# Summing the four scan states of the third layer's attention on DVE instead of POOL

## The reference, cut to what matters

```python
def step(state, inp):
    d, b, c, u = inp
    dA = jnp.exp(d[..., None] * A)
    state = state * dA + (d * u)[..., None] * b[:, None, :]
    y = jnp.einsum('bdn,bn->bd', state, c)
    return (state, y)
...
y = y + D[None, :, None] * x
y = y * silu(z)
```

## Time and profile before

| | us |
|---|---|
| median of 3 runs | 1397.1 |
| lowest and highest | 1387.31 and 1399.21 |
| the profiled execution | 1404.3 |
| its span in the profile | 1402.6 |
| PE busy in the span | 1117.5 (80%) |
| DVE busy | 849.2 (61%) |
| POOL busy | 690.5 (49%) |
| ACT busy | 619.9 (44%) |

### The profile page before, as it was taken

One profiled execution on the slowest core, in us unless ns is written; L12 is line 12 of the kernel. 1 busy time (PEld: TensorE's weight loads), 2 busy tenths in 40 slices (PEclk: granted clock), 3 DMA queues, 4 the chain that ended last, 5 costly groups with the idle time before them and its releaser, 6 DMA issues.

```text
span 1402.6 us, 18531 instructions
## 1 busy us (share of the span) xinstructions
PE 1117.5 (80%) x5412; PEld 855.1 (61%) x5413; DVE 849.2 (61%) x1510; ACT 619.9 (44%) x1682; POOL 690.5 (49%) x457
## 2 busy tenths in 40 slices
PE   6766598777635887998998999759899635999993
PEld 4545476666323565777777777645555334888782
DVE  4475998979668853787878787922222564332222
ACT  4383355454451116786786867642111115333330
POOL 1005888887301213796886886810000003788874
PEclk9678899999767998999999999989999856999997
DMA  5572899986510003121221211055100397455556
GB/s 171 159 145 85 220 264 288 272 217 131 124 27 0 1 1 98 42 83 43 83 70 55 67 57 54 7 156 131 36 0 0 108 243 196 78 82 82 82 83 128
DMA packets 131233, 146.11 MB, mean 104 GB/s; under 512 B 29654, under 2 KB 115407, under 8 KB 131159
## 3 DMA queue, kind: packets, MB, share of 16 engines
q1 hardware_dynamic: 105494, 110.58, 27.5%
q0 software_dynamic: 24576, 33.57, 14.3%
q10 hardware_dynamic: 1088, 1.05, 0.2%
HBM read 119.04 MB, written 26.12 MB: 103 GB/s over the span
## 4 chain that ended last, share of the span: by engine, by line
PE 44%; issue 16%; POOL 11%; DVE 10%; DMA 7%; SPq 6%; ACT 5%; another core or an unknown queue 1%; DVEq 0%; ACTq 0%; POOLq 0%
PE bank L1967 5%; PE bank L1567 4%; PE bank L2260 4%; PE bank L1545 3%; POOL f_sums L927 3%; POOL arena L913 3%; PE bank L1487 3%; PE bank L1976 3%; PE bank L1578 3%; SPq L2146 3%; PE bank L1476 2%; POOL y L2182 2%; PE bank L1505 2%; DMA e_sums<-ctxT,put 2%; PE bank L1278 2%
## 5 line engine op out<-in xcount | busy, mean ns | idle before, releaser
L200 POOL TENSOR_TENSOR rstd<-var_eps,minus_half 128x8 f32<-128x8 f32 x8 | 13.2, 1647 | 304.8 <-DVE var_eps L192 304.8
L478 DVE TENSOR_TENSOR_SCAN arena<-arena 128x1024 f32<-128x1024 f32 x64 | 152.8, 2388 | 13.4 <-issue 5.8
L927 POOL DMA_INDIRECT f_sums<-arena,put x64 | 122.0, 1907 | 26.4 <-issue 16.5
L913 POOL DMA_INDIRECT arena<-y_rows,slots x64 | 84.7, 1324 | 77.3 <-DVEq L1122 58.1
L2260 PE MATMUL bank<-arena,ssm_y 128*128 x512 | 111.8, 362 | 2.4 <-issue 1.0
L2173 POOL DMA_INDIRECT e_sums<-ctxT,put x64 | 101.6, 1587 | 23.8 <-issue 16.5
L456 ACT ACTIVATE arena<-arena,ssm_A 128x255 f32<-128x255 f32 (+1 forms) x256 | 108.1, 503 | 1.8 <-DVE arena L428 1.8
L1693 ACT ACTIVATE arena<-bank,x_nb,x_rq 128x256 f32<-128x256 f32 x128 | 71.0, 560 | 82.1 <-DVE x_nb L1768 81.3
L1967 PE MATMUL bank<-yT,arena 128*128 128x512 f32 (+1 forms) x224 | 102.2, 600 | 0.0
L508 PE MATMUL bank<-arena,ident 128*128 128x256 f32 x256 | 70.3, 422 | 38.1 <-DVE arena L498 34.6
L2182 POOL DMA_INDIRECT y<-y_rows,slots x64 | 62.8, 982 | 74.1 <-DMA y_rows<-y 52.9
(11 more groups left out here) (321 smaller groups left out, 2802.1 us busy)
## 6 DMA issues: line engine op xcount, KB each, us to landing
arena<-bc_rows SPq DMA_DIRECT2D x64, 512.0 KB
arena<-in_L_ffn_w_gate_dram SPq DMA_DIRECT2D x16, 256.0 KB
arena<-in_L_ffn_w_up_dram SPq DMA_DIRECT2D x16, 256.0 KB
arena<-in_L_ffn_w_down_dram SPq DMA_DIRECT2D x16, 256.0 KB
x<-in_L_ffn_w_gate_dram SPq DMA_DIRECT2D x16, 256.0 KB
y<-in_L_ffn_w_up_dram SPq DMA_DIRECT2D x16, 256.0 KB
yT<-in_L_ffn_w_down_dram SPq DMA_DIRECT2D x16, 256.0 KB
arena<-in_L_ffn_Wd_dram SPq DMA_DIRECT2D x1, 3072.0 KB, 23.6
```

The lines of the kernel that those rows point to most:

```text
L478: nc.vector.tensor_tensor_scan(ssm_h[:, j % 2, :], ssm_decay[:, j % 2, :], ssm_in, 0.0, ALU.mult, ALU.add).then_inc(s_ssm_h, 1)
L913: nc.gpsimd.indirect_dma_start(out=f0_xg[:, n % RING, e, :], out_offset=None, in_=y_rows, in_offset=bass.IndirectOffsetOnAxis(ap=slots[:, ...
L927: nc.gpsimd.indirect_dma_start(out=f0_sums[m % SUMS], out_offset=bass.IndirectOffsetOnAxis(ap=put[:, m:m + 1], axis=0), in_=f0_ye[:, n % R ...
```

## The change

`ssm_out_pool` and `ssm_out_dve` go. POOL keeps only the product with C. DVE gets `ssm_reduce_dve` in every even step (b = 0 and 2): it sums the four states of the group before with one `tensor_reduce` (1024 elements in, 256 out; the four values of a sum lie 256 elements, 1024 bytes, apart) into `ssm_part`, and adds that to `ssm_y` with one addition of 256 elements. It stands after `add` and `krms` and ahead of `mixed_copy`. The last group's sum is done at the end of the layer, where `ssm_out_dve` stood. POOL's product into a half of `ssm_hC_buf` waits for the reduction that read that half, by the same semaphore as before (`s_ssm_red`); the semaphore of the additions, `s_ssm_red_y`, now counts 32 instead of 8.

```diff
-        def ssm_out_pool(pool, m, b, j):
+        def ssm_reduce_dve(dve, m, b, j):
 
             c = j % HC
             q = b * GB * HC + j
-            ssm_hC(pool, nc.gpsimd, m, b, j)
-            pool.wait_ge(s_ssm_hC, m * GROUPS + q + 1)
-            add = nc.gpsimd.tensor_tensor
-            both = ssm_hC_buf[:, j % 2, 0:2 * S]
-            add(both, both, ssm_hC_buf[:, j % 2, 2 * S:4 * S], ALU.add).then_inc(s_ssm_half[0], 1)
...
-        def ssm_out_dve(dve, m, b):
-
-            for c in range(HC):
-                dve.wait_ge(s_ssm_red, b * GB * HC + (GB - 1) * HC + c + 1)
-                row = ssm_y[:, m, ds(b, 1), c, :].rearrange("p a l -> p (a l)")
-                nc.vector.tensor_tensor(row, row, ssm_acc[:, c, :], ALU.add).then_inc(s_ssm_red_y, 1)
+            dve.wait_ge(s_ssm_hC, m * GROUPS + q + 1)
+            if not (isinstance(b, int) and b == 0 and j == 0):
+                dve.wait_ge(s_ssm_red_y, q)
+            nc.vector.tensor_reduce(ssm_part[:, :], ssm_hC_buf[:, j % 2, :].rearrange("p (n l) -> p l n", n=NB),
+                                    AX_X, ALU.add).then_inc(s_ssm_red, 1)
+            dve.wait_ge(s_ssm_red, q + 1)
+            row = ssm_y[:, m, ds(b, 1), c, :].rearrange("p a l -> p (a l)")
+            nc.vector.tensor_tensor(row, row, ssm_part[:, :], ALU.add).then_inc(s_ssm_red_y, 1)
...
                 if b == 0 and not beyond(h + 1):
                     krms(h + 1)
-                if b == 1 and k == 0 and not (isinstance(i, int) and i == 0):
-                    ssm_out_dve(dve, 1, i - 1)
+                if b % 2 == 0 and ago >= 2:
+                    j = 2 * k + b // 2
+                    ssm_reduce_dve(dve, 1, i if j else i - 1, j - 1 if j else GB * HC - 1)
                 if ago >= 1:
                     mixed_copy(s - 1, (b - 1) % B)
...
-            ssm_out_dve(dve, 1, B - 1)
+            ssm_reduce_dve(dve, 1, B - 1, GB * HC - 1)
...
-                ssm_out_pool(pool, 1, i, 2 * k)
+                ssm_hC(pool, nc.gpsimd, 1, i, 2 * k)
...
-                ssm_out_pool(pool, 1, i, 2 * k + 1)
+                ssm_hC(pool, nc.gpsimd, 1, i, 2 * k + 1)
```

More of the change, by code:

```diff
@@ L562, in gated_dve @@
                 norm_dve(dve, k)
-                dve.wait_ge(s_ssm_red_y, B * HC)
+                dve.wait_ge(s_ssm_red_y, GROUPS)
             else:
@@ L1380, in flamingo_kernel @@
         x_ksq = area(2 * NT * P, NT, P)
-        ssm_acc = area(3 * NT * P, HC, S)
-        assert 3 * NT * P + HC * S <= l1_free + 2 * AR + K1 * A1
+        ssm_part = area(3 * NT * P, S)
+        assert 3 * NT * P + S <= l1_free + 2 * AR + K1 * A1
         x_gqk = sb("x_gqk", [P, 2])
@@ L1403, in flamingo_kernel @@
         s_x_vT, s_x_vTc, s_x_Mc = (s_l0_energy, B), (s_l0_attT, B), (s_l0_attTp, B)
-        s_ssm_half, s_ssm_some = (s_l0_out, B), (s_l0_att, B)
         def after(eng, sem_, value):
@@ L1923, in g_sp @@
         def g_sp(sp):
-            sp.wait_ge(s_ssm_red_y, B * HC)
+            sp.wait_ge(s_ssm_red_y, GROUPS)
             pad = FS2 // P * P
```

## The result

| | before | after |
|---|---|---|
| median, us (4 runs each, side by side) | 1397.43 | 1427.16 |
| lowest to highest, us | 1387.31 to 1399.21 | 1424.13 to 1435.45 |
| profiled execution, us | 1404.3 | 1427.05 |
| its span, us | 1402.6 | 1425.3 |
| plain head of the third layer, us | 21.68 | 24.04 |

The ratio is 1.0222, with a 95% interval from 1.0173 to 1.0271: the kernel became slower. In two later comparisons the kernel before had medians of 1401.93 (19 runs) and 1400.90 (11 runs), so the side-by-side difference of 29.7 us may in part be a low reading of before. The two profiled executions differ by 22.7 us.

A forecast was written before the change was run, and what follows sets the result against it. PE bounds the stage; DVE matters only where PE waits. 32.8 - 3.4 - 14.2 + 2.2 + 1.6 = 19.0 us, 1.35% on 1404.3, so 1416 us from the 1397.1 median; range 1390 to 1440.

The forecast's parts named there:

- likeliest case: Step b = 0 of 14 heads: DVE's addition waits for POOL's scaling, PE stands still 2.34 us; 1416 us, chance 0.52.
- The reduction: DVE's new reduction takes 1.91 us, like the strided reduction L2378, rather than 1.22 us.
- The race: Step b = 0: POOL's scaling starts at 4.94, DVE's addition could at 5.06; projection moves from 5.23 to 7.57 us.
- The head: Plain heads of 21.68 us gain PE's stop of 2.34 us; over 14 heads 32.8 us.
- old losses: Heads k = 1 lose scan's collision, 3.4 us off; heads k = 0 lose blocked additions and lower clock, 14.2.
- The step b = 2: DVE gains 1.34 us of work there, covered by its 1.73 us wait for PE, so no cost.
- The end: After head 14's stop of 2.34 us, three steps without PE cover add 2.2 us, the layer's last sum 1.6.
- The product: DVE's product L467 falls from 2.23 to 1.22 us in a plain step b = 0, with no POOL addition ahead.
- first rival: As forecast, and PE's clock also falls, in all 14 heads: 23.9 us more, 1440 us; chance 0.18.
- second rival: Step b = 0: addition gets in ahead of POOL's scaling, projection 0.70 us late; -4.0 us, 1393; chance 0.14.
- third rival: Reduction takes 1.22 us, so PE's projection in these heads starts as before; -16.7 us, 1380; chance 0.07.

The follow-up runs named there:

- second experiment: Kernel after, but the reduction adds four neighbouring values instead of the four states, so the sums are not the scan's: 1387.43 us, ratio 0.9874.
- first experiment: Kernel after, but POOL's scaling of the keys waits for DVE's addition of the same step: 1401.55 us, ratio 0.9995.
- fifth experiment: Kernel after, with DVE's loop over i = 1, 2 written out: 1421.30 us, ratio 1.0120.
- third experiments: Kernel after, but POOL's product stores the four states next to one another and the reduction reads neighbours: 1389.71 us, ratio 0.9925.

## Why the prediction was right, and where its sum fell short

The direction, the mechanism and the place were as forecast; 1427 lies in the range but 3 us above the likeliest case's own range (1408 to 1424). By the steps:

- **The reduction.** Forecast 1.91 us from the strided row, measured 1.94. The choice between that row and the product's 1.22 decided the sign, and the second experiment shows it: at 1.21 us the kernel is faster than before.
- **The race.** Forecast: scaling ahead by 0.12 us, addition's end 7.11 after the row maxima, projection at 7.57. Measured in head 3: 0.10, 7.08 (628.87 - 621.79) and 7.47. The first experiment reverses the order with the same work on DVE, and 1.66 of a plain head's 2.36 us are gone. That the addition is locked out, and not merely slow, is shown by the one that has a single column.
- **The head.** Forecast 24.02 (21.68 + 2.34), measured 24.04. Heads k = 0 and k = 1, at 24.24 and 23.98, are no longer different: their old losses are gone.
- **The step b = 2.** Forecast covered by 1.73 us with 1.34 added. Measured: 0.39 of the cover left, which is that difference.
- **The end.** Forecast 2.34 + 2.2 + 1.6 = 6.1 us from head 14 on, measured 6.2 (53.91 to 60.13 us, from b = 2 of head 13 to SP's first load of the next weights).
- **The product.** Forecast near 1.22 throughout; it is 1.20 to 1.23 in all 64.

The missing 7 us lie in heads 1 to 13. They took 299.19 us before and 319.32 after, 20.1 more, and the sum had 13 x 2.34 - 3.4 - 14.2 = 12.8. Heads 1 and 12 are 1.69 us longer than a plain head each, and head 8 is 3.58 longer, together 7.0 of the 7.3; the rest are differences of under 0.3 us in the other heads.

- **The clock** is the first rival, which was priced for all 14 heads and came true in two, heads 1 and 12. (In head 8 it fell as well, behind another stop.) In head 1 the stop looks like any other, and the products behind it took 3.31 us instead of 1.88:

```profile
579.49 1.13 PE L1562 MATMUL bank<-arena 128*128 128x256 f32 x4 [2.08 <-DVE arena L1727]
580.46 3.31 PE L1471 MATMUL bank<-yT,arena 128*128 128x512 f32 x4
653.50 1.13 PE L1562 MATMUL bank<-arena 128*128 128x256 f32 x4 [2.28 <-DVE arena L1727]
```

A stop of 2.08 us can thus be followed by the lower clock, and mostly isn't. Each fall cost 1.69, and 1.71 was the estimate. What sets the two heads apart is open, but it is not the length of the stop, by which the prediction judged: the last row is head 4, which stopped for 2.28 us and kept the full clock (1.00). In the kernel before with two memsets, too, head 4 stopped for 2.81 us and kept it, while the same stop of 2.81 us in the kernel before was followed by the lower clock (26.41 us, 0.94):

```profile
627.61:652.37 24.76, 21.26 (x117) 17.00 (x116) 21.96 (x43) 17.30 (x55) 21.35 (x13) 1.00 0.20 60
649.63 1.12 PE L1579 MATMUL bank<-arena 128*128 128x256 f32 x4 [2.81 <-DVE arena L1744]
```

The prediction gave all or nothing; a share of the heads would have been the better form.

- **The way back of DVE's loop** was in no step and no rival. The prediction listed what the change adds to DVE by its busy time, and left out what a changed loop body could cost where the loop goes back. That the branch back is where it happens is shown, since the wait goes when the loop is written out. The Trainium skill has a rule for it: its page "Runtime: NRT & Kernel Launch", section "Instruction fetch mechanics", says that a taken branch to a target which is not among the instructions held must fetch it before the engine goes on. The runs agree as far as they go: 2.81 us at the branch, none without it. But that DVE waits there for instructions is argued and not shown, since the profile names nothing, and why the loop of the kernel before, even when longer, goes back without a wait is not settled. The second wait, which the expectation of the fifth experiment puts at 2 us, was 1.03 in the kernel after.

With the falls in heads 1 and 12 and with head 8, whose 3.58 us are the way back and a fall together (PE is busy there for 22.80 us as against 21.26), the sum is 19.0 + 3.4 + 3.6 = 26.0. Both terms are read off this trace, so that is book-keeping and no test. The stage (from b = 2 of head 0 to the load of the next weights) grew from 353.10 to 379.45 us, by 26.35. The profiled executions differ by 3.6 less, in other stages that the change doesn't touch. Single executions of the kernel before range from 1387 to 1410 us, so nothing can be read from that.

Head 8 brings the other cases nearer, too. The second rival gave -4.0; with the 3.77 us that head 8 is longer in the first experiment's trace (26.15 against 22.38, at a clock of 0.93) it is -0.2, and that experiment measured -0.4. The third rival's -16.7 becomes -13.0 with the way back's 3.72, and the second and third experiments measured -14.5 and -12.2. The intervals of these three are 5 to 9 us to either side, so an agreement in tenths is luck.

## What to carry to other kernels

Before DVE is given work with two inputs in SBUF, work out which instruction of POOL runs at that moment and which of the two starts first: here 0.10 us of lag cost 1.66 us in each plain head (24.04 against 22.38 with the order turned), and that POOL was busy for half as long was not seen in the time. If DVE must add up several parts, let the producer store them next to one another, so that the reduction is short enough to be ahead; a wait that puts POOL behind is the second best. And after adding instructions to a loop, look at its way back for idle time marked "issue".

## What the runs showed of the hardware that was not expected

- POOL's instruction does not shut DVE out whenever it runs. In the second experiment the addition takes its free 0.42 us (622.79 to 623.21) wholly inside POOL's power of 8 elements (621.72 to 623.36), and so it does in all 14 heads there and in both runs with the states innermost (0.43 us at most), while the same addition waits out the scaling of 1024 elements. The Trainium skill's page "SBUF — State Buffer", section "Who interferes with whom", lets an instruction of DVE with two SBUF inputs contend with one of POOL that reads SBUF, and makes the order of issue decide, with the pair of ports held for a whole instruction. The first experiment agrees with the order, and the scaling does hold to its end; the rows of the power show no lock for the whole of an instruction, as far as POOL's spans, which the profile gives only roughly, can be trusted.
- A stride of 1024 bytes in what DVE's reduction reads cost 1.94 us against 1.21, about as much as the smaller strides of the earlier trace rows (1.88 and 1.91). A stride of 16 bytes in what POOL's product writes cost 0.03 us.
- Going back to the start of the changed kernel's loop cost DVE 2.81 us of idle time marked "issue" and 1.03 us more a little later, with the states innermost 2.81 and 1.17; there it made the head 3.7 us longer at full clock. In the loop of the kernel before it cost nothing that the profile shows.
- A stop of PE of the same 2.81 us was followed by the lower clock in one run (26.41 us, 0.94) and not in another (24.76 us, 1.00), in the same head.
